# Layer 1's cross-attention in quarters of 512 queries, shorter prologue, ternary sums on TensorE, SiLU a block ahead

## The chip, the cores and the metric

The kernel runs on one core of one Trainium2 chip, in one launch. The metric is the device time of an execution in microseconds (us); what is quoted is the median over several executions. TensorE does matmuls (PE in the profile, PEld its weight loads), VectorE is DVE, ScalarE is ACT, GpSimd is POOL, and SyncE (SP) issues the transfers.

## What is computed

1024 tokens of width 128 (`x`) go through two layers, with a context of 6404 rows of width 96. Every sublayer is `x = layernorm(x + f(x))`.

```
layer 0: linear attention, 16 heads (relu, rms-normed q and k)
         cross-attention on the context, 8 heads of 64, softmax over 6404 keys
         mixture of experts: 64 routed of 88 wide (top 8), 2 shared, silu(x Wg) * (x Wu)
layer 1: attention with rotated q, k, v (1024 x 1024 softmax)
         BitNet cross-attention:
             vis = bit(ctx, W_d2v); img = bit(vis, W_img); fused = bit(x, W_txt)
             for r in (0, 1):                        # two rounds
                 kv = bit(img, W_att[r])             # 6404 x 64
                 k = concat(kv, kv)                  # 6404 x 128
                 attn = softmax(fused k^T / sqrt(128))
                 fused = fused + 0.1 * attn k
             h = relu(bit(concat(fused, mean(img)), W_f1)); out = bit(h, W_f2)
         low-rank experts (top 2 of 8), and a last layernorm
bit(x, W): ws = mean|W|, qW = sign(W) * (|W| > ws / 2); is = max|x| / 127
           out = (round(x / is) @ qW^T) * (ws * is) + b
```

As `k` holds `kv` twice, a round's scores are the product of `kv` with the sum of the two halves of `fused`. A matrix DUP of the kernel, in one matmul, makes that sum and doubles it onto both halves of the 128 rows.

## The kernel before

**Precision.** A float32 product is made of float16 parts (high and low), in three matmuls: low keys by high queries, high by low, high by high. The exponentials and the values are float32, in matmuls that take several passes.

**Scores in place.** The PSUM banks of the scores are not cleared from tile to tile. The keys are stored as differences from the key some tiles before (256 earlier, the constant LAG), so that each matmul adds what turns the last scores into the next. A half begins with "seeds" (L1855), matmuls that put minus the query's maximum into the banks by a diagonal matrix.

**The maximum.** The maximum over the keys is wanted before the exponentials. It is taken over pairs of keys, as (sum + |difference|): TensorE makes both products for 512 or 1024 keys (L1833 and L1838 in a pass "alone", L1917 between other work), ScalarE takes the magnitude (L774 and L778, L815), VectorE adds the two and reduces (L1180). The pass alone is `max_alone`; beside other work it goes step by step, and a step's TensorE part waits for VectorE's of the step before the last.

**Layer 0's cross-attention** runs in eight halves (`hf`, 512 queries by two heads each), in four pairs `p`. A half has 26 units of two key tiles; each tile has scores (L1870) on two bank pairs, exp by ScalarE (L795), values by TensorE (L1885). The sums of the exponentials for the denominators are shared by VectorE (`add_up`, L1230) and GpSimd (L606), GpSimd with a quarter of the columns. Beside this, in "slots", the next pair's sums, keys and values are made (`items_of`, all through bank 5, one item freeing the bank for the next: `FREED_BY`), and its maxima. Layer 1's context path runs beside it too (`CHAIN`, on VectorE; `BIT_AT` lists at which slots of the first pair the ternary weights are made). It has two reductions across partitions by GpSimd: L617 (the sum of the rows' |W| in the first half) and L614 (the maximum `AM` in the third half); they stand between GpSimd's sums of these halves.

**Prologue.** Transfers of x and of the context in 7 chunks; the first linear attention (L1746 to L1767); context high parts by ScalarE (L714), low parts by VectorE (three, L1081) and GpSimd (L569); differences between the two halves of the keys by GpSimd (L562), their rounding by ScalarE (L724); the first LayerNorm; first values, sums and keys through banks 3 to 7 (`K16_EARLY` and `V_EARLY` of them ahead of the queries); then the first maximum alone (L1833).

**Experts.** 46 blocks of 128 rows: 44 of routed experts, 2 of shared. For block n: up and gate matmuls (L2058), SiLU by ScalarE (L928), products by VectorE (L1415, L1421), a float16 high part by ScalarE (L941), the low part by GpSimd (L636), down matmuls. ScalarE's order in the loop is

```
hidden_hi(4 * i + j, j)
silu(4 * i + (1 + j), (1 + j) % 2)
```

**Layer 1's cross-attention** has two rounds. Each: a DUP matmul pair (L2190) of XT, the fused state with features on the partitions; the queries' high part by ScalarE (L1004) and low part by VectorE (L1614); a maximum alone of 26 steps (`ALONE1`), seeds, 26 units of two tiles by 1024 queries with sums on VectorE 1024 wide for each tile; denominators (L1897), reciprocal (L1236), normalization (L1245). Then VectorE scales the four blocks into `OO` (L1632) and adds them to XT (L1636), 1024 wide. Beside the first round the second's keys (`dk`), values and sums ("sides") are made, through banks 6 and 7 and bank 5. GpSimd quantizes the mean of the image embeddings (L648, L649) between all-reduces of the later quantizations; it gives a bias for `h` (L2217). TensorE has 43 matmuls there that only keep it going (L1713).

## Time and profile before

| what | us |
|---|---|
| median of 3 executions (lowest, highest) | 1700.82 (1698.92, 1707.68) |
| profiled execution, its time | 1697.55 |
| profiled execution, its span | 1695.8 |
| TensorE busy in the span | 1547.2 (91%) |
| VectorE busy | 1300.1 (77%) |
| ScalarE busy | 1111.2 (66%) |
| GpSimd busy | 432.4 (25%) |
| mean granted TensorE clock, share of full speed | .938 |

The span is that of the instructions of the core; the execution's time is 1.75 us more. Stages by the trace: prologue to 71.9, layer 0's cross-attention to about 1035, experts from 1052 to about 1270, layer 1's attention and quantizations to 1361.8, its cross-attention to 1640.04 (the last denominators), the tail to 1695.8. In a row, the first number is the start from the start of the span, the second the time that the merged instructions (x8: eight of them) took; in brackets the idle time of the engine before and what ended it.

### The profile page before, as it was taken

To read this page: it belongs to the slowest core of one execution; us is meant where nothing else is said; L and a number is where in the kernel's file an instruction comes from. 1 tells how busy PE (TensorE), PEld (TensorE's weight loads), DVE (VectorE), ACT (ScalarE), POOL (GpSimd) and SP (SyncE) were. 2 spreads that over 40 slices of the span, in tenths; PEclk is the share of its full clock that TensorE was granted. 3 is DMA by queue.
4 is the path that set the end of the run, shared out by engine and by line. 5 is a ranking of instruction groups with operands and counts; after the bars stand their busy time and mean duration, and the time that the engine had idled before them with its cause. 6 is when DMAs were issued, how large, how long until landed. Compare 5 with 4: busy or idle time off the path is not lost.

```text
span 1695.8 us, 26434 instructions
## 1 busy us (share of the span) xinstructions
PE 1547.2 (91%) x9040; PEld 557.2 (33%) x9058; DVE 1300.1 (77%) x2233; ACT 1111.2 (66%) x1490; POOL 432.4 (25%) x407
## 2 busy tenths in 40 slices
PE   6888899999989999999999998999997969978996
PEld 4412223333323333333332333333444612211333
DVE  7798888779877778887788888766665686778775
ACT  5587777767867767877777786655553366746543
POOL 6203433434533434434400010344441000000000
PEclk8758999999999999999999998999999969976998
DMA  4000000000100000000010000111100000000000
GB/s 130 7 1 6 1 1 1 1 2 12 48 8 1 1 2 3 1 1 10 20 33 1 1 1 26 33 43 46 42 23 1 1 1 1 1 0 1 1 13 13
DMA packets 14829, 22.75 MB, mean 13 GB/s; under 512 B 1990, under 2 KB 11766, under 8 KB 14710
## 3 DMA queue, kind: packets, MB, share of 16 engines
q1 hardware_dynamic: 14710, 21.22, 4.5%
q8 instruction: 68, 1.11, 0.3%
q14 instruction: 51, 0.42, 0.1%
HBM read 20.69 MB, written 0.52 MB: 13 GB/s over the span
## 4 chain that ended last, share of the span: by engine, by line
PE 66%; issue 13%; DVE 12%; POOL 5%; ACT 3%; DMA 0%; POOLq 0%; SPq 0%; DVEq 0%; ACTq 0%
PE PS L1885 26%; PE PS L1870 18%; PE PS L1917 5%; POOL WRK L636 4%; DVE KNB L1180 4%; PE PS L1833 3%; PE PS L1739 2%; PE PS L1731 2%; DVE WRK L1230 1%; DVE QS L1236 1%; PE PS L2164 1%; ACT KNB L815 1%; PE PS L2149 1%; PE PS L1855 1%; PE PS L1723 1%
## 5 line engine op out<-in xcount | busy, mean ns | idle before, releaser
L1230 DVE TENSOR_TENSOR WRK<-WRK 128x768 f32<-128x768 f32 (+1 forms) x500 | 549.3, 1099 | 60.2 <-ACT WRK L795 45.2
L795 ACT ACTIVATE WRK<-PS 128x1024 f32<-128x1024 f32 (+1 forms) x510 | 500.0, 1023 | 108.1 <-PE PS L1870 89.9
L1885 PE MATMUL PS<-WRK,V 128*64 128x512 f32 (+1 forms) x2040 | 495.0, 605 | 0.0
L1180 DVE CUSTOM_DVE_ANT_0 KNB<-PS,KNB 128x512 f16<-128x512 f32 (+2 forms) x464 | 331.3, 731 | 127.1 <-PE PS L1917 114.9
L606 POOL TENSOR_TENSOR WRK<-WRK 128x256 f32<-128x256 f32 x300 | 282.3, 941 | 395.5 <-ACT WRK L795 378.3
L815 ACT ACTIVATE KNB<-PS 128x512 f16<-128x512 f32 (+2 forms) x306 | 180.7, 591 | 97.3 <-PE PS L1917 97.2
L2058 PE MATMUL PS<-WRK,KNB 128*128 128x512 f16 x828 | 197.1, 383 | 12.7 <-POOL WRK L636 4.3
L1885 PEld LDWEIGHTS PS<-WRK,V 128*64 128x64 f32 (+1 forms) x2040 | 124.1, 136 | 246.6 <-issue 199.8
L1870 PE MATMUL PS<-Q,KB 64*128 64x512 f16 (+1 forms) x1428 | 192.8, 379 | 0.1
L1870 PE MATMUL PS<-KNB,KB 64*128 64x512 f16 (+1 forms) x1224 | 155.7, 376 | 0.0
L636 POOL TENSOR_TENSOR WRK<-KB,WRK 128x1024 f16<-128x1024 f32 x46 | 98.6, 2144 | 132.6 <-ACT WRK L941 132.6
L2058 PEld LDWEIGHTS PS<-WRK,KNB 128*128 128x128 f16 x828 | 77.1, 98 | 124.0 <-issue 23.4
L774 ACT ACTIVATE KNB<-PS 128x1024 f16<-128x1024 f32 x96 | 98.0, 1024 | 27.0 <-DVE MXP L1180 15.5
L1415 DVE TENSOR_TENSOR KA<-PS,KB 128x1024 f32<-128x1024 f32 x46 | 56.3, 1225 | 72.7 <-ACT KB L928 72.7
L1870 PEld LDWEIGHTS PS<-Q,KB 64*128 64x128 f16 (+1 forms) x1428 | 65.5, 94 | 129.1 <-ACT WRK L795 44.7
L941 ACT ACTIVATE WRK<-KB 128x1024 f16<-128x1024 f32 x46 | 48.6, 1057 | 90.4 <-DVE KB L1421 87.1
L645 POOL PARTITION_ALL_REDUCE AM<-AX x3 | 1.1, 370 | 378.3 <-DVE AX L1641 293.8
L1917 PE MATMUL PS<-KNB,Q 64*128 64x512 f16 (+1 forms) x448 | 79.4, 357 | 17.9 <-DVE MXP L1180 10.0
L1870 PEld LDWEIGHTS PS<-KNB,KB 64*128 64x128 f16 (+1 forms) x1224 | 59.7, 94 | 62.8 <-issue 10.9
L1833 PE MATMUL PS<-CTX,Q 64*128 64x512 f16 x192 | 49.9, 598 | 15.4 <-DVE MXP L1180 7.4
L1870 PE MATMUL PS<-Q,KA 64*128 64x512 f16 (+1 forms) x408 | 62.3, 384 | 0.0
L1833 PE MATMUL PS<-KNB 64*128 64x512 f16 x192 | 49.8, 604 | 11.5 <-DVE MXP L1180 7.2
(347 smaller groups left out, 1532.1 us busy)
## 6 DMA issues: line engine op xcount, KB each, us to landing
V<-in_moe_w_dram SPq DMA_DIRECT2D x44, 192.0 KB, 2.4
KNB<-in_ctx_fm_dram SPq DMA_DIRECT2D x6, 384.0 KB, 8.2
X<-in_ctx_fm_dram SPq DMA_DIRECT2D x12, 192.0 KB, 2.4
CTX<-in_ctx_fm_dram SPq DMA_DIRECT2D x6, 384.0 KB, 3.9
BW<-in_bit_w_dram SPq DMA_DIRECT2D x1, 960.0 KB, 10.0
PWK<-in_pair_w_dram SPq DMA_DIRECT2D x4, 192.0 KB, 2.4
XT<-in_x_fm_dram SPq DMA_DIRECT2D x1, 512.0 KB, 4.6
X<-in_x_tm_dram SPq DMA_DIRECT2D x1, 512.0 KB, 11.6
```

The source lines that it names most:

```text
L606: e.tensor_tensor(total, total, part, ALU.add).then_inc(S("acc_pool"), 1)
L636: e.tensor_tensor(H_LO[hslot], MH[hslot % 2], H_HI[hslot], ALU.subtract).then_inc(S("h_lo"), 1)
L774: e.activation(MC[:, m % 2, :], bank(b, b + 2), ACT.Abs).then_inc(S("x_cp"), 1)
L795: e.activation(PR[0:r, u % 2, b, :], bank(2 * b, 2 * b + 2, slice(0, r)), ACT.Exp).then_inc(S("exp"), 1)
L815: e.activation(MC[:, m % 2, 0:w], PS[:, 6, 0:w], ACT.Abs).then_inc(S("x_cp"), 1)
L1180: return e.tensor_tensor_reduce(diffs, sums, diffs, 0.5, NEG, ALU.add, ALU.max, accum_out=out)
L1230: e.tensor_tensor(total, total, part, ALU.add).then_inc(S("acc"), 1)
L1833: ins = e.matmul(o, queries[rows, tiles[0] * P:(tiles[0] + 1) * P], keys[rows, at:at + HALF], start=True, stop=True)
L1870: ins = e.matmul(PS[0:r, 2 * b + h, :], keys[rows, j * P:j * P + r], queries[rows, q[h]], start=False, stop=(k == 2), skip_group_check=True)
L1885: ins = e.matmul(PS[h * HD:(h + 1) * HD, 4, :], v(r, j, h), PR[0:r, unit_no(hf, i) % 2, b, h * HALF:(h + 1) * HALF], start=(j == 0), stop= ...
L1917: ins = e.matmul(PS[:, b, k * w:(k + 1) * w], QH[(p + 1) % 2][rows, t * P:(t + 1) * P], K16[rows, off + a:off + a + w], start=True, stop=True)
L2058: ins = e.matmul(bank(b + h), w_[:, part, :], rows[:, h * HALF:(h + 1) * HALF], start=start and i == 0, stop=stop and i == 2, skip_group_c ...
```

## The change

It has six parts.

1. **Layer 1's cross-attention in quarters.** The quarter n is round n // 2 and the query half n % 2. A unit of a quarter is two key tiles on the two halves of the rows, by 512 queries. The maximum of the first quarter alone is taken in 13 steps (`ALONE1`); those of the next three in 26 steps of half the width (`STEPS1`) beside the units of the quarter before: in quarter 0 in units 0 to 23, in quarters 1 and 2 in units 7 to 23 (`steps1`), with up to two steps in a unit. There are four buffers for the exponentials (PR1) for two before. Round 1's sides, values and keys go one a unit through bank 5 (`items1_of`). A quarter's denominators, normalization, a DUP matmul on it ("fold") and its addition to half of XT run in the next quarter's units 1 to 4, and the query matmul of the quarter after next in unit 6. GpSimd adds 0.1 times the bias to XT ahead. The keys of layer 1 are differences from 512 earlier.
2. **Prologue.** GpSimd makes all of the context's remainders and two small weight remainders; two groups of first values go early, by banks 6 and 7; first keys go through five banks; fewer sums and values stand ahead of the queries; R's bias is added by GpSimd.
3. **Ternary sums** across partitions by a matmul with ones in slot 12 of the first pair ("bits"), VectorE copies the result. The all-reduce for AM[0] stands after all of GpSimd's sums of layer 0.
4. **The mean** is quantized by VectorE.
5. **Layer 1's text quantization** loses its clamp: two VectorE operations for three.
6. **Experts:** on ScalarE SiLU of block n + 1 stands ahead of the high part of block n.

The core of the diff:

```diff
-ALONE1 = full_then_rest(NDC - 1, lambda t: (t % 2,), 6)
+ALONE1 = [(d, [t], t % 2) for d in range(NDC - 1) for t in range(NT // 2)] + [(NDC - 1, [0, 1, 2, 3], 0)]
...
+    if p == 0:
+        at[12].append(("bits", 0))
     at[27].append(("den", 2 * p))
...
+STEPS1 = [(c, [t], t % 2) for c in range(NFULL) for t in range(NT // 2)] + [(NFULL, [0, 1, 2], 0), (NFULL, [3], 1)]
+NM1 = len(STEPS1)
...
+def steps1(n, i):
+    first, last = (0 if n == 0 else 7), NU - 3
+    if n + 1 == QUARTERS or not first <= i <= last:
+        return []
+    k = last - first + 1
+    return list(range((i - first) * (NM1 + 1) // k, (i - first + 1) * (NM1 + 1) // k))
+def items1_of(n):
+    at = {i: [] for i in range(NU)}
+    if n == 0:
+        for k, x in enumerate(SIDES):
+            at[k].append(("side", x))
+        for k, x in enumerate(NEXT_KV[:NU - len(SIDES)]):
+            at[len(SIDES) + k].append(x)
+    else:
+        at[1].append(("den", n - 1))
+        at[2].append(("den2", n - 1))
+        at[4].append(("fold", n - 1))
+        if n < 3:
+            at[6].append(("query", n + 1))
+        if n == 1:
+            for k, x in enumerate(NEXT_KV[NU - len(SIDES):]):
+                at[0 if k == 0 else 7 + k].append(x)
+    return at
...
-K16_EARLY, V_EARLY = 14, 6
+K16_EARLY, V_EARLY = 12, 5
...
-            q.dma_start(PWK[:, :, :], pair_w[0, :, 0:3, :]).then_inc(S("ld_pwk"), 16)
+                if c == 3:
+                    q.dma_start(PWK[:, :, :], pair_w[0, :, 0:3, :]).then_inc(S("ld_pwk"), 16)
...
             difference(2)
+            remainder(0)
+            remainder(1)
+            e.wait_ge(S("wk_hi"), 1)
+            e.tensor_tensor(WK3[0:DC, 1, :], PWK[0:DC, 1, :], WK3[0:DC, 0, :], ALU.subtract).then_inc(S("wk_lo"), 1)
+            e.wait_ge(S("wv_hi"), 1)
+            e.tensor_tensor(WV2[0:DC, 1, :], PWK[0:DC, 2, :], WV2[0:DC, 0, :], ALU.subtract).then_inc(S("wv_lo"), 1)
             difference(3)
+            remainder(2)
             remainder(3)
             for c in range(4, NKC):
                 difference(c)
...
+            e.wait_ge(S("ln_x"), NT)
+            e.tensor_tensor(R[:, :, :], X_[:, :, :], sm("bo").unsqueeze(1).to_broadcast([P, NT, D]),
+                            ALU.add).then_inc(S("r_bias"), 1)
...
-                    if hf == 2 and i == MAG_DONE + 1:
-                        e.wait_ge(S("ax"), 1)
-                        e.partition_all_reduce(AM[:, 0:1], AX[:, 0:1], P, RED.max).then_inc(S("am"), 1)
-                    if hf == 0 and i == 11:
-                        e.wait_ge(S("bit_rows"), 1)
-                        e.partition_all_reduce(BT[:, 0:7], BR[:, 0:7], P, RED.add).then_inc(S("bit_sum"), 1)
-            for i in range(1, 3):
+            for i in range(3):
                 e.wait_ge(S("ax"), i + 1)
                 e.partition_all_reduce(AM[:, i:i + 1], AX[:, i:i + 1], P, RED.max).then_inc(S("am"), 1)
             link(e.memset(SWAP, 0.0))
             for base in (0, HD, -HD):
                 diag(DUP, base)
             e.sem_inc(S("dup"), 1)
+            for r in range(2):
+                link(e.tensor_scalar(BT1[:, r:r + 1], sm(f"b_att{r}"), 0.1, None, ALU.mult))
             e.wait_ge(S("ln_x"), 2 * NT)
...
             for i in range(3, 6):
+                if i == 4:
+                    add_bias(0, 0, slice(0, T))
...
+                        add_bias(quarter, 1, slice((quarter - 1) * HALF, quarter * HALF))
                 e.wait_ge(S("ax"), i + 1)
                 e.partition_all_reduce(AM[:, i:i + 1], AX[:, i:i + 1], P, RED.max).then_inc(S("am"), 1)
-                if i == 4:
-                    e.wait_ge(S("ws"), 5)
-                    link(e.tensor_scalar(AVG[:, 0:1], AVG[:, 1:2], AI[:, 4:5], MAGIC, ALU.mult, ALU.add))
-                    e.tensor_scalar(AQ[:, :], AVG[:, 0:1], MAGIC, None, ALU.subtract).then_inc(S("avg_q"), 1)
...
-            for c in range(NKC):
+            for c in range(4):
                 context_hi(c)
             k_weights(0)
             v_weights(0)
+            for c in range(4, NKC):
+                context_hi(c)
...
-            e.wait_ge(S("ctx_dve"), DVE_DIFF + DVE_LO)
-            e.wait_ge(S("c_lo"), 1)
+            e.wait_ge(S("c_lo"), 4)
...
                         weights_hi(4 * i + (2 + j), j, 16 * i + (48 if j >= 2 else 16))
+                    silu(4 * i + (1 + j), (1 + j) % 2)
                     hidden_hi(4 * i + j, j)
-                    silu(4 * i + (1 + j), (1 + j) % 2)
...
+                t = turn(n, i)
+                e.wait_ge(S("sc"), BEFORE_SC + t + 1)
+                if t >= len(PR1):
+                    e.wait_ge(S("pv"), BEFORE_PV + t - len(PR1) + 1)
+                    e.wait_ge(S("acc"), BEFORE_SC + t - len(PR1) + 1)
+                b = 2 * (i % 2)
...
+            for n in range(QUARTERS):
                 for i in range(NU):
-                    for b in tiles_of(i):
-                        exp(hf, i, b)
-                    if r == 0:
-                        beside((NEXT_KV, lambda x: kv(1, x)), i, NU)
-                        if i < len(SIDES):
-                            sums_and_differences(1, *SIDES[i], 5)
-                copy_out(hf)
+                    magnitude1(n, steps1(n, i)[0:1])
+                    exp1(n, i)
+                    magnitude1(n, steps1(n, i)[1:])
+                    if i == 0 and n:
+                        copy_out1(n - 1)
+                    for x in ITEMS1[n][i]:
+                        bank5_1(x)
...
-                e.wait_ge(S("c_hi"), c + 1)
-                split_lo(C_LO[0:DC, a:a + w], CTX32[:, a:a + w], C_HI[0:DC, a:a + w]).then_inc(S("ctx_dve"), 1)
-            k_weights(0)
-            v_weights(0)
+            for g in range(2):
+                first_values(g, first_values_bank(g))
...
+                first_values(g, first_values_bank(g))
             q_out(0, 0, 2)
             q_out(0, 1, 7)
             for g in range(V_EARLY, NVG):
-                first_values(g, 3 + g % 3)
-            e.tensor_tensor(R[:, :, :], X_[:, :, :], over_tiles(sm("bo")), ALU.add).then_inc(S("a0_dve"), 1)
+                first_values(g, first_values_bank(g))
             for c in range(NKP):
-                k_out(0, c, 3 + (NVG + c) % 3)
+                k_out(0, c, first_keys_bank(c))
...
                     e.wait_ge(S("bit_sum"), 1)
+                    e.tensor_copy(BT[:, 0:7], PS[:, 5, 0:7]).then_inc(S("bit_dve"), 1)
+                    e.wait_ge(S("bit_dve"), 1)
...
-            quantize(XQ, bank(0, 2), XF, 3).then_inc(S("quant"), 1)
+            link(e.tensor_scalar(XF, bank(0, 2), AI[:, 3:4], MAGIC, ALU.mult, ALU.add))
+            e.tensor_scalar(XQ, XF, MAGIC, None, ALU.subtract).then_inc(S("quant"), 1)
...
+            def add_up1(n, i):
+                t = turn(n, i)
+                e.wait_ge(S("exp"), BEFORE_SC + t + 1)
+                r, w = (P, T) if len(tiles_of(i)) > 1 else (TAIL, HALF)
+                part = PR1[t % len(PR1)][0:r, 0:w]
+                if i:
+                    e.wait_ge(S("acc"), BEFORE_SC + t)
+                    total = ACC[0:r, n % 2, 0:w]
+                    e.tensor_tensor(total, total, part, ALU.add).then_inc(S("acc"), 1)
+                else:
+                    e.wait_ge(S("den_ps"), 2 * PAIRS + n - 1)
...
+            def fold(n):
+                r, u = divmod(n, 2)
+                part = slice(u * HALF, (u + 1) * HALF)
+                e.wait_ge(S("fold"), n + 1)
+                e.wait_ge(S("pre_b"), 1 if r == 0 else 2 + u)
+                e.scalar_tensor_tensor(XT[:, part], bank(5), 0.1, XT[:, part], ALU.mult,
+                                       ALU.add).then_inc(S("fused_upd"), 1)
...
-            e.tensor_tensor(AX[:, 4:5], AVG[:, 2:3], AVG[:, 3:4], ALU.max).then_inc(S("ax"), 1)
+                    maximum1(quarter, steps1(quarter, i)[0:1])
+                    if i:
+                        add_up1(quarter, i - 1)
+                    elif quarter:
+                        add_up1(quarter - 1, NU - 1)
+                    maximum1(quarter, steps1(quarter, i)[1:])
+                    for x in ITEMS1[quarter][i]:
+                        bank5_1(x)
+                    if quarter + 1 < QUARTERS and i == NU - 2:
+                        shifts1(quarter + 1)
...
+            link(e.tensor_scalar(AVG[:, 0:1], AVG[:, 1:2], AI[:, 4:5], MAGIC, ALU.mult, ALU.add))
+            e.tensor_scalar(AQ[:, :], AVG[:, 0:1], MAGIC, None, ALU.subtract).then_inc(S("avg_q"), 1)
...
+                elif kind == "bits":
+                    e.wait_ge(S("bit_rows"), 1)
+                    e.matmul(PS[:, 5, 0:7], ones[:, :], BR[:, 0:7], start=True, stop=True).then_inc(S("bit_sum"), 1)
...
+            def fold(n):
+                e.wait_ge(S("on"), 2 * PAIRS + n + 1)
+                e.matmul(bank(5), DUP, ON[:, n % 2 * HALF:(n % 2 + 1) * HALF], start=True,
+                         stop=True).then_inc(S("fold"), 1)
...
+            def max_steps1(n, steps):
+                base = base1(n)
+                for m in steps:
+                    if m == 0:
+                        e.wait_ge(S("f2_lo"), max(n, 1))
+                        e.wait_ge(S("lk16"), (n // 2 + 1) * 2 * NSC)
+                    if m < NM1:
+                        e.wait_ge(S("x_cp"), base + m)
+                    e.wait_ge(S("mx"), base + m - 1)
+                    if m < NM1:
+                        max_half1(n, m, 0, 6, "x_ps")
+                    if m:
+                        max_half1(n, m - 1, NH, 7, "y_ps")
...
+            for n in range(QUARTERS):
+                if n == 2:
+                    e.wait_ge(S("lk_lo"), 2 * NKP)
+                    e.wait_ge(S("vt_ev"), 2 * NVT)
                 for i in range(NU):
-                    for b in tiles_of(i):
-                        scores(hf, i, b)
+                    max_steps1(n + 1, steps1(n, i)[0:1])
+                    scores1(n, i)
+                    max_steps1(n + 1, steps1(n, i)[1:])
+                    for x in ITEMS1[n][i]:
+                        bank5_1(x)
                     if i:
-                        for b in tiles_of(i - 1):
-                            values(hf, i - 1, b)
-                    if r == 0:
-                        beside((NEXT_KV, lambda x: kv(1, x)), i, NU)
-                        if i < len(SIDES):
-                            sums_and_differences(1, *SIDES[i], 5, 1)
-                values(hf, NU - 1, 0)
-                denominators(hf)
+                        values1(n, i - 1)
+                    elif n:
+                        values1(n - 1, NU - 1)
+            values1(QUARTERS - 1, NU - 1)
+            denominators1(QUARTERS - 1)
+            fold(QUARTERS - 1)
```

## Rows read from the trace of the kernel before

**Rows 1.** The page: the chain that ended last, by engine.

```profile
PE 66%; issue 13%; DVE 12%; POOL 5%; ACT 3%; DMA 0%; POOLq 0%; SPq 0%; DVEq 0%; ACTq 0%
```

**Rows 2.** Windows: busy us (instructions) of PE, PEld, DVE, ACT, POOL; PEclk, DMA, GB/s.

```profile
183.00:189.00 6.00, 5.29 (x34) 1.41 (x30) 5.18 (x10) 4.38 (x7) 1.74 (x3) 1.00 0.00 1
...
1366.00:1400.00 34.00, 25.07 (x112) 4.67 (x112) 30.44 (x65) 27.00 (x28) 0.00 (x0) 0.57 0.00 1
```

**Rows 3.** Timelines (start, us, engine, line) in layer 1's attention; last: a group.

```profile
1369.24 1.22 DVE L1180 CUSTOM_DVE_ANT_0 KNB<-PS,KNB 128x1024 f16<-128x1024 f32 x1
...
1371.74 1.22 DVE L1180 CUSTOM_DVE_ANT_0 KNB<-PS,KNB 128x1024 f16<-128x1024 f32 x1
...
1401.62 1.89 PE L1855 MATMUL PS<-DIAG,ones 128*128 128x512 f16 x4 [2.92 <-DVE DIAG L1207]
...
1502.72 1.08 PE L1897 MATMUL PS<-WRK,ones 128*64 128x512 f32 x4
...
1552.94 1.89 PE L1855 MATMUL PS<-DIAG,ones 128*128 128x512 f16 x4 [2.92 <-DVE DIAG L1207]
...
1629.89 0.39 PE L1870 MATMUL PS<-Q,KB 64*128 64x512 f16 x2
...
1633.16 0.39 PE L1870 MATMUL PS<-Q,KB 64*128 64x512 f16 x2
...
1640.04 1.08 PE L1897 MATMUL PS<-WRK,ones 128*64 128x512 f32 x4
...
L1230 DVE TENSOR_TENSOR WRK<-WRK 128x1024 f32<-128x1024 f32 x24 | 29.4, 1225 | 9.8 <-ACT WRK L795 8.6
```

**Rows 4.** Timelines of TensorE and VectorE in a slot of layer 0.

```profile
183.83 0.39 PE L1917 MATMUL PS<-KNB,Q 64*128 64x512 f16 x2
...
184.06 0.81 PE L1870 MATMUL PS<-KNB,KB 64*128 64x512 f16 x6
...
184.29 0.69 DVE L1180 CUSTOM_DVE_ANT_0 KNB<-PS,KNB 128x512 f16<-128x512 f32 x1 [0.19 <-PE PS L1917]
...
185.13 0.39 PE L1917 MATMUL PS<-KNB,Q 64*128 64x512 f16 x2 [0.27 <-DVE MXP L1180]
...
189.34 0.39 PE L1917 MATMUL PS<-KNB,Q 64*128 64x512 f16 x2
```

**Rows 5.** Timelines of GpSimd and TensorE around the two all-reduces.

```profile
201.69 8.79 POOL L606 TENSOR_TENSOR WRK<-WRK 128x256 f32<-128x256 f32 x8 [7.05 <-issue]
...
205.04 0.39 PE L1917 MATMUL PS<-KNB,Q 64*128 64x512 f16 x2 [3.46 <-issue]
...
496.53 0.71 POOL L606 TENSOR_TENSOR WRK<-WRK 4x256 f32<-4x256 f32 x1 [7.01 <-issue]
...
497.39 1.98 PE L1897 MATMUL PS<-WRK,ones 128*64 128x512 f32 x4 [4.68 <-POOL WRK L606]
```

**Rows 6.** Timelines of TensorE and ScalarE over one expert block.

```profile
1241.22 2.75 PE L2058 MATMUL PS<-WRK,KNB 128*128 128x512 f16 x12 [0.19 <-ACT KB L928]
...
1244.59 1.01 ACT L928 ACTIVATE KB<-PS 128x1024 f32<-128x1024 f32 x1
...
1249.11 1.01 ACT L928 ACTIVATE KB<-PS 128x1024 f32<-128x1024 f32 x1
```

**Rows 7.** Timelines of GpSimd, ScalarE and VectorE in the prologue.

```profile
25.17 5.81 POOL L562 TENSOR_TENSOR WRK<-KNB 96x1024 f32<-96x1024 f32 x3
...
35.79 1.11 ACT L688 ACTIVATE KNB<-PS 128x512 f16<-128x512 f32 x2 [0.95 <-PE PS L1724]
...
35.05 2.21 DVE L1081 TENSOR_TENSOR WK<-PWK,WK 96x128 f16<-96x128 f32 x1
...
37.18 0.76 DVE L1081 TENSOR_TENSOR WV<-PWK,WV 96x128 f16<-96x128 f32 x1
```

**Rows 8.** Timeline of TensorE after layer 1's last denominators.

```profile
1645.23 10.31 PE L1713 MATMUL PS<-BQ,ones_b 128*128 128x512 bf16 x43 [0.22 <-issue]
...
1658.40 0.25 PE L2217 MATMUL PS<-AQ,BQ 128*128 128x1 bf16 x4 [2.86 <-POOL AQ L649]
```

424 lines of the change are left out of this document (285 added, 139 removed).

## The prediction, made before the changed kernel ran

> **What bounds the kernel now.** I read the page first: TensorE is busy 91% of the 1695.8 us, and the chain that ended last runs through it for 66% and through VectorE for 12% [rows 1]. So an edit pays where TensorE waits, or where it loses work or clock. The windows show its granted clock [rows 2], and the timelines of the edited stretches where it waits: layer 1's attention [rows 3], a slot of layer 0 with the maximum beside it [rows 4], GpSimd around its all-reduces [rows 5], an expert's block [rows 6], the prologue [rows 7] and the tail [rows 8]. In the attention TensorE starts work back to back: a unit of 2 key tiles by 1024 queries takes 3.27 us (1629.89 to 1633.16). The time beside that is the two passes for the maximum, 50.2 us for the second with what leads to it (1502.72 to 1552.94). Durations are of one profiled execution of 1697.55 us, 3.3 below the median of 1700.82; I add the sum to the first and put the 3.3 back.
>
> **Layer 1's attention.** The stretches of before are seeds to denominators, 101.1 us (1401.62 to 1502.72) and 87.1 us (1552.94 to 1640.04), with 50.2 between. *Removed:* the second pass alone, and 13 of the first one's 26 steps. Two steps take 2.50 us (1369.24 to 1371.74) [rows 3], so the seeds come 13 x 1.25 = 16.3 us earlier, at 1385.3.
> *Added on TensorE:* 188.2 us of the two stretches stay. 104 half-units replace 51, each of half of that unit's 3.27 us, 1.635, and, my estimate, .055 for the extra changes of tile shape: +5.7. The 78 steps for the next quarter's maximum cost .23 each (183.83 to 184.06, the pair of matmuls [rows 4]): +17.9. Three more denominators of four float32 matmuls, twice the old ones' four passes (1.08 with their fill, .94 each without, by my estimate), 1.87 each: +5.6. The fold of each quarter and the query of two, single float32 matmuls of half of 1.87: 5 x .93 = +4.7. Round 1's keys, values and sides through the one bank 5, where the key pieces must wait for their eviction: +2.5. Waiting for the queries: +1.4. Sum 226.0 us.
> *Added as a wait:* one item's maximum needs TensorE, then VectorE, and TensorE's next step needs the bank back. In a unit with two steps I see this ring: .46 from TensorE's step to VectorE's start (183.83 to 184.29), .62 for the first maximum (.69, less what overlaps with the next instruction) [rows 4], then a 1024-wide sum of 1.15 (1.225 in the group's mean, less the overlap of neighbours [rows 3]), then the second maximum, .84 from its start to TensorE's next step (184.29 to 185.13). 3.07 us, where TensorE's own work in such a unit is 1.69 + 2 x .22 = 2.13. Quarters 1 and 2 have ten two-step units each, as the steps are squeezed into 17 of 26 units: 20 x .94 = 18.8; quarter 0 has three, already longer by their keys: 2.0; and seven key pieces of quarter 1 in the same units .5 each: 3.5. Sum 24.3. Behind the waiting step stand the scores, and behind those the exponentials, so nothing fills it. That layer 0 shows the like speaks for it: a slot with three steps takes 5.51 us (183.83 to 189.34) [rows 4], and TensorE waits in it for the maximum (.27 before 185.13).
> So the last denominators start at 1385.3 + 226.0 + 24.3 = 1635.6 instead of 1640.04: **-4.4**. Were the ring hidden: -28.7.
>
> **Ternary sums by TensorE, AM's first all-reduce later.** GpSimd goes away before each all-reduce and behind it: 7.05 us before its next sum at 201.69, 7.01 before 496.53 [rows 5]. The sum that comes late holds a buffer of the exponentials, so TensorE then waits 3.46 (before 205.04); the second time 4.68 (before 497.39). Removed: 3.5 and 4.7, and an estimated .8 for the matmuls that run slowly behind the second (1.98 us for four of 1.08 [rows 3, 5]). Added: a float32 matmul of 7 columns at slot 12 and VectorE's copy that frees bank 5, for which the key matmul of slot 13 waits; a TensorE-VectorE-TensorE trip like the .84 above, about 1 us. The AM all-reduce now stands behind GpSimd's last sum of layer 0 on its queue; VectorE asks for it one or two slots later, so I cost it at nothing; without that cover it is one spell, 7. Sum **-8**; bounds -11 (all idle gone, clock kept) and 0 (the spell comes back at the fourth pair).
>
> **Experts.** A block takes 4.52 us (SiLU 1244.59 to 1249.11). It is a ring: ScalarE's rounding of block n waits for VectorE, SiLU of n + 1 (1.01) stands behind it, and VectorE's two products wait for SiLU, the four of about the same length, and so the sum of a block [rows 6]. With SiLU of the next block first the ring is open; but TensorE idles just .19 us in a block (before 1241.22), so it binds next at 4.33: 43 x .2 = **-8.6**. Bounds: -11 (the drain shortens too) and +2 (product late by a SiLU, 1.01, for the down matmuls, which stand two blocks behind; only the last block pays).
>
> **Prologue.** GpSimd takes VectorE's three remainders and the small weights' two. Its differences, 5.81 us for three [rows 7], gate ScalarE's halves, and these stand on ScalarE's queue ahead of the sums' evictions (35.79). They end 3 x 1.94 + 2 x .5, 7 us later, or 11 if each of the remainders is half as long again. In return VectorE and ScalarE enter the LayerNorm sooner, five value and key evictions, each a little above half of 1.11 [rows 7], no longer stand ahead of the queries (-3.2), R's bias leaves VectorE's queue and the keys go through five banks. The queries were ready late anyway. The normalization starts .6 late; sum **-1.5**, bounds -3.5 and +4 (the 7 to 11 less those covers).
> The Trainium skill ("SBUF — State Buffer", section "SBUF: two separate sides") has VectorE and GpSimd exclude one another on a shared port for a whole instruction. A 96x128 subtraction of VectorE took 2.21 us beside GpSimd's wide one, the same shape right behind .76 [rows 7], so the trace agrees. By the rule GpSimd alone would be at its short time and the prologue nearer -3.
>
> **Rest.** Layer 1's text quantization loses one of three 1024-wide VectorE passes: -.7. The first key piece of round 0 needs one matmul for three: -.2. Mean quantized by VectorE: the query-independent matmul waited 2.86 us for GpSimd (before 1658.40). But the 43 matmuls that keep the clock up (10.31 us) stand ahead of it [rows 8], and they now start after the last fold. From the last denominators: 2.0 to VectorE, 3.4 for the reciprocals, .7, fold 1.0, transposes 1.1, then 10.3: 18.7 against 18.4 (1640.04 to 1658.40). **+.4**, bounds -3 and +3.
>
> Sum: -4.4 - 8 - 8.6 - 1.5 - .7 - .2 + .4 = -23.0: 1674.6, and 3.3 more for the median, **1678**. Its own range, by the terms' bounds apart from the ring: 1666 to 1690.
>
> **Rivals.** A. *The ring is hidden* (VectorE's maximum slips before the sum, or the four probability buffers absorb it): attention -28.7, time 1653. For: the chain in rows 4 also shows a two-step stretch, and TensorE there is busy 5.29 of 6 us [rows 2]. Against: the 5.51 us slot. Chance .24; a ring half hidden (1666) is the lower end of my case.
> B. *Experts don't gain*, because GpSimd or TensorE's weight loads stand at 4.5 already: 1686. Chance .10.
> C. *The clock falls in the quarters.* With TensorE idle .94 of 3.07 us in ten units running, the granted clock may go to 1.2 GHz, as where the first pass alone runs it shows a mean of .57 with TensorE busy 25 of 34 us [rows 2]. A two-step unit then takes 2 x 2.13 = 4.26, 1.19 more than the ring; in 20, with the one-step units of these quarters (14 x 1.9), +50: 1728. It makes the kernel slower from about two thirds of them (1678 + 33 = 1711). Against: rows 2's stretch at 183 us, clock 1.00 with idle of this size. Chance .07.
> D. *The moved work pays itself back*: the prologue's differences at +4, the all-reduce late by 7 and quarters at +6: 1696 to 1705, no change. .10.
> My case .49. That the change doesn't do what it says is excluded: the diff removes the second pass and both all-reduces.
>
> **How the numbers follow.** Range: from A, less 2 for its other terms (1651), to the near end of D (1694). A measurement of this kernel can tell about .5%, 8.5 us, from no change. Faster holds my case, A and B but for a tail: .81; within .5%: D and that tail, .11; slower: C and what of D exceeds, .08.
>
> **What would show it.** Right: one pass of thirteen wide steps; two-step units of quarters 1 and 2 at about 3.07 us with TensorE's maximum step waiting for VectorE; no idle of 6 to 7 us on GpSimd in pairs 0 and 1, and no exponential waiting over 2 us there; blocks of 4.3 us; the first maximum step near 70.4; the mean's matmul right behind the 43. Wrong: two-step units near 2.2 us (A), blocks of 4.5 (B), a granted clock under .9 in 1420 to 1600 (C), a first maximum step past 74 or a new wait at the fourth pair (D).

## The result and the profile after

The changed kernel takes 1673.73 us (median of 4; 1672.37 to 1674.18), the kernel before beside it 1701.57: the ratio is 0.983, with a 95% interval of [0.9803, 0.9857], 27.8 us less. The forecast was 1678. The profiled execution has a span of 1672.3 us for 1695.8, 23.5 less, where the working had 23.0; the other 4 us lie between that execution of before and the median beside which it is now held.

The page of the changed kernel, its busy times:

```profile
PE 1544.0 (92%) x9078; PEld 556.9 (33%) x9096; DVE 1301.9 (78%) x2306; ACT 1121.4 (67%) x1531; POOL 442.5 (26%) x415
```

TensorE is about as busy as before (1544.0 us for 1547.2) in a shorter span. What went is nearly all waiting. To see where, I read the same landmarks in both traces: when a group of matmuls starts. The last column splits the prediction's terms over the same stretches.

| stretch, by TensorE's landmarks | before | after | difference | forecast |
|---|---|---|---|---|
| start to the first maximum | 71.87 | 68.46 | -3.4 | -1.5 |
| to layer 0's first seeds | 67.00 | 67.00 | 0 | 0 |
| to the 1st denominators (ternary sums) | 118.80 | 118.31 | -.5 | -2.5 |
| to the 4th (AM's all-reduce is in the 3rd) | 373.95 | 368.26 | -5.7 | -5.5 |
| to the 8th | 401.84 | 401.86 | 0 | 0 |
| to the filler behind the experts | 248.30 | 233.87 | -14.4 | -8.6 |
| to the DUP matmuls | 80.02 | 82.14 | +2.1 | -.9 |
| to layer 1's first seeds | 39.84 | 22.99 | -16.9 | -16.3 |
| to its last denominators | 238.42 | 253.37 | +15.0 | +11.9 |
| to the end | 55.76 | 56.04 | +.3 | +.4 |

**The quarters.** Timelines of TensorE and VectorE in the third quarter (start, us, engine, line; they answer to [rows 3, 4]):

```profile
1525.13 0.39 PE L2457 MATMUL PS<-CTX,Q 64*128 64x512 f16 x2
...
1525.59 0.69 DVE L1311 CUSTOM_DVE_ANT_0 KNB<-PS,KNB 128x512 f16<-128x512 f32 x1 [0.16 <-PE PS L2457]
...
1526.21 1.22 DVE L1767 TENSOR_TENSOR WRK<-WRK 128x1024 f32<-128x1024 f32 x1
...
1526.44 0.39 PE L2457 MATMUL PS<-CTX,Q 64*128 64x512 f16 x2 [0.27 <-DVE MXP L1311]
...
1527.35 0.69 DVE L1311 CUSTOM_DVE_ANT_0 KNB<-PS,KNB 128x512 f16<-128x512 f32 x1
...
1528.19 0.39 PE L2457 MATMUL PS<-CTX,Q 64*128 64x512 f16 x2 [0.34 <-DVE MXP L1311]
...
1530.17 0.39 PE L2457 MATMUL PS<-CTX,Q 64*128 64x512 f16 x2
```

From TensorE's first step (1525.13) to VectorE's maximum are .46 us, then .62 to the sum, 1.14 to the second maximum and .84 to TensorE's step of 1528.19: the ring is 3.06 us, and the prediction had 3.07. That closing step is the first one of the next unit, which has one step; the two units together take 5.04 (1525.13 to 1530.17), where the prediction had 3.07 + 1.91. A unit without steps takes 1.76 in the last quarter, where I had 1.69.

**The all-reduces.** GpSimd has none left in layer 0's first five halves; the first stands at 846.3 us, behind its last sum of layer 0. The new item, and the wait for VectorE's copy that it brings to TensorE (.39 and .91 us, 1.3 together):

```profile
189.20 0.39 PE L2162 MATMUL PS<-BR,ones 128*128 128x7 f32 x2
...
194.19 0.39 PE L1925 MATMUL PS<-CTX,WK 96*128 96x512 f16 x1 [0.91 <-DVE BT L1434]
```

**The experts.** The selector matmuls, one pair a block, and ScalarE in the same stretch (they answer to [rows 6]):

```profile
1237.20 0.59 PE L2285 MATMUL PS<-KA 128*128 128x512 f16 x2
...
1241.52 0.59 PE L2285 MATMUL PS<-KA 128*128 128x512 f16 x2
...
1240.42 1.02 ACT L1012 ACTIVATE KB<-PS 128x1024 f32<-128x1024 f32 x1 [0.71 <-PE PS L2262]
...
1241.34 1.05 ACT L1025 ACTIVATE WRK<-KB 128x1024 f16<-128x1024 f32 x1
```

4.32 us a block; SiLU now waits for TensorE (.71 before 1240.42), and the high part follows it. TensorE has no idle left in a block. The last up and gate matmuls, in the drain behind the last block (before, then after):

```profile
1278.82 2.74 PE L2058 MATMUL PS<-WRK,KNB 128*128 128x512 f16 x6 [3.04 <-POOL WRK L636]
```

```profile
1256.24 1.47 PE L2262 MATMUL PS<-WRK,KNB 128*128 128x512 f16 x6 [1.49 <-POOL WRK L712]
```

The wait is 1.55 us shorter, and the six matmuls behind it are 1.27 shorter, as they ran slowly in the kernel before.

**Prologue and tail.** GpSimd and the first maximum step (compare [rows 7]), the tail's filler and the mean's matmul (compare [rows 8]):

```profile
18.38 4.22 POOL L639 TENSOR_TENSOR CTX<-KNB,CTX 96x1024 f16<-96x1024 f32 x2
...
22.56 0.42 POOL L646 TENSOR_TENSOR WK<-PWK,WK 96x128 f16<-96x128 f32 x1
...
30.82 4.80 POOL L632 TENSOR_TENSOR WRK<-KNB 96x1024 f32<-96x1024 f32 x3
...
68.46 1.02 PE L2037 MATMUL PS<-KNB 64*128 64x512 f16 x6 [1.51 <-DVE KB L1217]
...
1625.33 9.81 PE L1915 MATMUL PS<-BQ,ones_b 128*128 128x512 bf16 x43 [0.22 <-issue]
...
1634.97 0.24 PE L2523 MATMUL PS<-AQ,BQ 128*128 128x1 bf16 x4
```

GpSimd's first remainders take 2.1 us each (4.22 for two), the small weight's .42 where VectorE's took 2.21 [rows 7]. The mean's matmul stands right behind the 43.

One edit of the prologue is not in the list of six parts: the reciprocals of the first linear attention's q and k go to PSUM and no longer to SBUF. VectorE's two products with them take 2.35 us for 6.64 (L1273, before L1137). In this profile VectorE then waits 8.39 us for ScalarE ahead of the normalization, so these 4.3 us are not seen to arrive at the first maximum by themselves; no run takes the edit out.

**The clock.** In two places the same matmuls take longer than in the profile of the kernel before: behind the first seeds and behind the experts. In windows of all engines (columns as in [rows 2]), first the kernel before:

```profile
134.00:146.00 12.00, 8.31 (x43) 2.75 (x41) 7.48 (x36) 6.39 (x11) 1.12 (x2) 0.68 0.00 1
...
1281.70:1300.00 18.30, 16.21 (x112) 9.43 (x112) 11.90 (x34) 8.36 (x12) 0.00 (x0) 1.00 0.00 1
...
1300.00:1322.00 22.00, 17.83 (x91) 10.64 (x89) 13.24 (x18) 9.42 (x14) 0.00 (x0) 0.92 0.00 1
...
1345.00:1362.00 17.00, 13.23 (x64) 6.48 (x65) 14.31 (x55) 2.83 (x12) 0.38 (x1) 1.00 0.00 0
```

Then the changed one, whose three windows behind the experts answer to those three:

```profile
134.00:146.00 12.00, 10.54 (x42) 3.50 (x44) 6.59 (x10) 6.66 (x12) 2.16 (x4) 0.70 0.00 0
...
1257.70:1276.00 18.30, 16.52 (x95) 9.25 (x95) 10.30 (x33) 7.58 (x11) 0.00 (x0) 0.91 0.01 1
...
1276.00:1298.00 22.00, 17.39 (x95) 10.03 (x96) 14.21 (x17) 9.54 (x14) 0.00 (x0) 0.92 0.00 1
...
1322.00:1341.00 19.00, 16.38 (x75) 8.46 (x76) 14.55 (x56) 3.88 (x13) 0.38 (x1) 0.91 0.00 0
```

The twelve score matmuls behind the seeds took 1.95 us from 140.66 in the kernel before. Here they, the queries' matmuls and those behind the experts:

```profile
137.26 2.74 PE L2074 MATMUL PS<-KNB,KB 64*128 64x512 f16 x12
...
139.93 2.62 PE L1919 MATMUL PS<-XT,PWK 128*128 128x512 f32 x4
...
1267.44 3.41 PE L2328 MATMUL PS<-XT,RQK 128*128 128x512 f32 x4
...
1284.56 3.45 PE L2368 MATMUL PS<-WRK,XT 128*128 128x512 f32 x4
...
1333.21 4.96 PE L1915 MATMUL PS<-BQ,ones_b 128*128 128x512 bf16 x16
```

2.74 us from 137.26, and the queries behind them 2.62 for 1.98: 1.4 us. The granted clock rises 2.8 us behind the seeds (138.87) in the kernel before and 5.8 behind them (135.46) here. That is not the edit's doing as far as the runs show: in run 3 below, whose prologue is that of the kernel before, it rises 5.7 behind them, and 4.5 to 5.9 in all the other profiles. The profile of the kernel before is the one apart.

Behind the experts four float32 matmuls take 3.41 (1.98 before), four more 3.45 (2.84 before), the filler 4.96 (3.62 before). The granted clock is .91, .92 and .91 in the three windows; in the kernel before it is 1.00, .92 and 1.00, so one of the three falls was there already. The stretch is 2.1 us longer, and with the .7 that the dropped pass should have given it, 2.8 us are lost.

### The profile page after: what moved, and what is told of

It reads as the page before. It is cut to its first block, busy times and chain, and to the rows that moved or that the text cites. A ratio compares the mean times of both kernels' runs of the same rounds, so it can differ in the third digit from the quotient of the medians.

```text
span 1672.3 us, 26773 instructions
## 1 busy us (share of the span) xinstructions
PE 1544.0 (92%) x9078; PEld 556.9 (33%) x9096; DVE 1301.9 (78%) x2306; ACT 1121.4 (67%) x1531; POOL 442.5 (26%) x415
## 4 chain that ended last, share of the span: by engine, by line
PE 63%; issue 14%; DVE 12%; POOL 6%; ACT 4%; POOLq 0%; DMA 0%; DVEq 0%; ACTq 0%; SPq 0%
PE PS L2088 21%; PE PS L2074 14%; POOL WRK L712 5%; PE PS L2120 5%; PE PS L2429 4%; DVE KNB L1311 4%; PE PS L2416 3%; PE PS L1941 2%; PE PS L1933 2%; PE PS L2037 2%; DVE WRK L1361 2%; DVE WRK L1767 1%; PE PS L2457 1%; DVE QS L1367 1%; ACT KNB L898 1%
## 5 line engine op out<-in xcount | busy, mean ns | idle before, releaser
L1361 DVE TENSOR_TENSOR WRK<-WRK 128x768 f32<-128x768 f32 (+3 forms) x400 | 426.9, 1067 | 14.4 <-ACT WRK L878 7.2
L878 ACT ACTIVATE WRK<-PS 128x1024 f32<-128x1024 f32 (+1 forms) x408 | 400.9, 1022 | 52.1 <-PE PS L2074 44.8
L2088 PE MATMUL PS<-WRK,V 128*64 128x512 f32 (+1 forms) x1632 | 395.6, 605 | 0.0
L2088 PEld LDWEIGHTS PS<-WRK,V 128*64 128x64 f32 (+1 forms) x1632 | 99.2, 136 | 194.1 <-issue 158.3
L2074 PE MATMUL PS<-Q,KB 64*128 64x512 f16 (+1 forms) x1224 | 152.6, 377 | 0.0
L1098 ACT ACTIVATE WRK<-PS 128x1024 f32<-128x1024 f32 x100 | 102.3, 1023 | 51.8 <-PE PS L2416 48.4
L1767 DVE TENSOR_TENSOR WRK<-WRK 128x1024 f32<-128x1024 f32 (+1 forms) x100 | 119.8, 1198 | 10.0 <-ACT WRK L1098 8.9
L2429 PE MATMUL PS<-WRK,V 128*64 128x512 f32 (+1 forms) x408 | 111.9, 617 | 0.3 <-DVE MXP L1311 0.3
L2120 PE MATMUL PS<-KNB,Q 64*128 64x512 f16 (+1 forms) x448 | 79.3, 357 | 14.6 <-DVE MXP L1311 10.1
L2074 PEld LDWEIGHTS PS<-Q,KB 64*128 64x128 f16 (+1 forms) x1224 | 55.5, 94 | 89.1 <-ACT WRK L878 21.1
L857 ACT ACTIVATE KNB<-PS 128x1024 f16<-128x1024 f32 x60 | 61.2, 1023 | 16.6 <-DVE MXP L1311 9.5
L1012 ACT ACTIVATE KB<-PS 128x1024 f32<-128x1024 f32 x46 | 47.1, 1023 | 35.7 <-PE PS L2262 35.7
## 6 DMA issues: line engine op xcount, KB each, us to landing
BW<-in_bit_w_dram SPq DMA_DIRECT2D x1, 960.0 KB, 10.1
```

Source lines behind the costliest of these rows:

```text
L878: e.activation(PR[0:r, u % 2, b, :], bank(2 * b, 2 * b + 2, slice(0, r)), ACT.Exp).then_inc(S("exp"), 1)
L1361: e.tensor_tensor(total, total, part, ALU.add).then_inc(S("acc"), 1)
L1767: e.tensor_tensor(total, total, part, ALU.add).then_inc(S("acc"), 1)
L2074: ins = e.matmul(PS[0:r, 2 * b + h, :], keys[rows, j * P:j * P + r], queries[rows, :], start=False, stop=(k == 2), skip_group_check=True)
L2088: ins = e.matmul(PS[h * HD:(h + 1) * HD, 4, :], V[0:r, j, h * HD:(h + 1) * HD], PR[0:r, unit_no(hf, i) % 2, b, h * HALF:(h + 1) * HALF], s ...
L2120: ins = e.matmul(PS[:, b, k * w:(k + 1) * w], QH[(p + 1) % 2][rows, t * P:(t + 1) * P], K16[rows, off + a:off + a + w], start=True, stop=True)
```

## The experiments

Each starts from the changed kernel where nothing else is said, and is held against its 1673.73. That was measured beside 1701.57 for the kernel before. Beside runs 1, 2, 6 and 7 the kernel before took 1700.34, beside 3, 4, 5 and 8 1699.62, and beside 9 1703.26: differences of 2 us and less between medians of different groups show nothing by themselves, and I go by the stages of the profiles there.

**1. Is VectorE's sum in the ring?** The two maxima of a unit ahead of the sum:

```diff
-                    maximum1(quarter, steps1(quarter, i)[0:1])
+                    maximum1(quarter, steps1(quarter, i))
                     if i:
                         add_up1(quarter, i - 1)
                     elif quarter:
                         add_up1(quarter - 1, NU - 1)
-                    maximum1(quarter, steps1(quarter, i)[1:])
```

> The changed kernel, but in a unit with two steps VectorE takes both maxima ahead of the 1024-wide sum. Theory 1 (the sum stands in the ring, as the prediction has it): a two-step unit with the one-step unit behind it takes 5.04 us in the third quarter of the changed kernel; without the sum in the ring TensorE's second step still waits for the first maximum (.46 + .62 + .23 = 1.31 from step to step), so the pair goes to 4.6 to 4.85, 3 to 7 us off the whole, and the seven key units gain most. Theory 2 (VectorE is simply full, or ScalarE's magnitude binds): pair stays at 5.04, total within 1 us. Theory 3 (whole ring gone): pair 4.04 to 4.2, total 15 to 20 us less.

Measured: 1670.83 us, ratio to the kernel before 0.983 [0.9813, 0.9846]. TensorE and VectorE in the third quarter:

```profile
1520.52 0.39 PE L2456 MATMUL PS<-CTX,Q 64*128 64x512 f16 x2
...
1521.98 1.22 DVE L1767 TENSOR_TENSOR WRK<-WRK 128x1024 f32<-128x1024 f32 x1
...
1523.12 0.68 DVE L1311 CUSTOM_DVE_ANT_0 KNB<-PS,KNB 128x512 f16<-128x512 f32 x1
...
1523.96 0.39 PE L2456 MATMUL PS<-CTX,Q 64*128 64x512 f16 x2 [0.42 <-DVE MXP L1311]
...
1525.29 0.39 PE L2456 MATMUL PS<-CTX,Q 64*128 64x512 f16 x2
```

The three steps of a pair of units go from 5.04 to 4.77 us (1520.52 to 1525.29), in the range of the first theory. The sum was in the ring; but taken out of one unit it delays the first maximum of the next (the sum of 1521.98 runs until 1523.12, TensorE's step waits .42). The third quarter, denominators to denominators, goes from 65.17 to 63.71 us, the second stays (68.04 and 68.07): 1.5 us in all, less than the 3 to 7 that I gave, and the key units gain nothing. The rest of the 2.9 lies where nothing was edited: the start (67.58 for 68.46), the stretch from there to the 1st denominators (.6 less) and the one behind the experts (81.46 for 82.14). Against the kernel before beside it, the ratio is that of the changed kernel, .983; so the medians alone don't show this gain, and the 1.5 us rest on one profile of each.

**2. Is the experts' period the ring through ScalarE?** SiLU behind the high part again:

```diff
-                    silu(4 * i + (1 + j), (1 + j) % 2)
                     hidden_hi(4 * i + j, j)
+                    silu(4 * i + (1 + j), (1 + j) % 2)
```

> The changed kernel with the experts' old order on ScalarE (high part of block n, then SiLU of n + 1). Theory 1 (the ring through VectorE and ScalarE made the old period): the spacing of the blocks goes from 4.32 back to a repeating 4.52, 4.52, 4.61, 4.67 (mean 4.58), 11 us over 43 blocks, and the drain behind the last block is 3 us longer; of that 2 us come back behind, if the granted clock in layer 1's attention then has fewer dips: total +12 to +14. Theory 2 (the prediction's size): +8.6. Theory 3 (the period fell because of something else, such as GpSimd): no change.

Measured: 1683.81 us, +10.1, less than the 12 to 14 that the first theory gave; the stretch to the filler is 246.43 us for 233.87, +12.6. Blocks and wait are back:

```profile
1247.69 0.60 PE L2285 MATMUL PS<-KA 128*128 128x512 f16 x2
...
1249.78 2.75 PE L2262 MATMUL PS<-WRK,KNB 128*128 128x512 f16 x12 [0.19 <-ACT KB L1012]
...
1252.36 0.59 PE L2285 MATMUL PS<-KA 128*128 128x512 f16 x2
```

4.67 us here, one of the repeating four (4.52, 4.52, 4.61, 4.67). The 43 periods give 11.0 of the 12.6. The drain gives 1.6, as TensorE waits 3.04 us in it again; the 3 us that I expected of it held another 1.3 for slow matmuls, and here the six behind that wait take 1.47. The stretch behind the filler is 79.59 us for 82.14, 2.5 less: the first four float32 matmuls take 1.98 again and the last filler 3.62.

**3. The same edit alone, on the kernel before.**

> The kernel before with nothing changed but the experts' order on ScalarE (SiLU of block n + 1 ahead of the high part of block n). Theory 1: blocks at 4.32 us for a mean of 4.58, the drain 3 us shorter, 14 us up to the first filler behind the experts, and 0 to 3 us of it lost to a lower granted clock in layer 1's first attention: total -11 to -14. Theory 2 (the prediction's size): -8.6. Theory 3 (the period also needs the other parts): less than 5.

Measured: 1685.59 us beside 1699.62, ratio 0.9909 [0.9893, 0.9924]: -14.0. The stretch to the filler is 234.93 us for 248.30, -13.4, and 80.26 for 80.02 behind it. The first theory holds for the edit. What it said of the clock does not hold as a price of the edit: here the stretch behind the filler lost .2, in the changed kernel 2.8.

**4. Did TensorE wait for GpSimd's all-reduces?** Both back on GpSimd, in the first and third half:

```diff
-        at[12].append(("bits", 0))
...
+                    if hf == 2 and i == MAG_DONE + 1:
+                        e.wait_ge(S("ax"), 1)
+                        e.partition_all_reduce(AM[:, 0:1], AX[:, 0:1], P, RED.max).then_inc(S("am"), 1)
+                    if hf == 0 and i == 11:
+                        e.wait_ge(S("bit_rows"), 1)
+                        e.partition_all_reduce(BT[:, 0:7], BR[:, 0:7], P, RED.add).then_inc(S("bit_sum"), 1)
```

> The changed kernel, but the ternary sums are reduced by GpSimd in the first half again and AM's first all-reduce stands in the third half again. Theory 1 (GpSimd is away for 6 to 7 us before and behind each, and TensorE waits for it): against the changed kernel the first denominators come 1.5 to 2.5 us later, the third's another 4.7 and the fourth's another .9; total +7 to +8.5, GpSimd's rows show 6 us before and 7 us behind each all-reduce. Theory 2 (the old waits had another cause, such as the exponentials' buffers): no such steps, total within 2 us.

Measured: 1682.20 us, +8.5. Around the first all-reduce:

```profile
190.59 0.49 POOL L695 PARTITION_ALL_REDUCE BT<-BR  x1 [5.92 <-issue]
...
198.54 6.16 POOL L684 TENSOR_TENSOR WRK<-WRK 128x256 f32<-128x256 f32 x6 [7.46 <-issue]
...
201.89 0.61 PE L2123 MATMUL PS<-KNB,Q 64*128 64x512 f16 x2 [3.78 <-issue]
...
202.27 2.79 PE L2077 MATMUL PS<-KNB,KB 64*128 64x512 f16 x12
...
205.42 2.90 PE L2091 MATMUL PS<-WRK,V 128*64 128x512 f32 x8
```

```profile
196.00:206.00 10.00, 6.22 (x28) 1.99 (x28) 4.72 (x12) 5.43 (x7) 6.17 (x7) 0.73 0.00 0
```

```profile
196.00:206.00 10.00, 6.54 (x44) 2.05 (x42) 6.36 (x19) 5.11 (x9) 3.73 (x5) 1.00 0.00 0
```

5.9 us before it and 7.5 behind, TensorE waits 3.78, as the first theory has it. But this half costs 3.9 us (122.19 from seeds to denominators for 118.31), more than the 1.5 to 2.5: behind the wait the twelve score matmuls take 2.79 us for 1.46 and the values 2.90 for 1.94, at a granted clock of .73. The second window is that of the kernel before, whose profiled execution kept the clock at 1.00 with its wait of 3.46. That is no property of the kernel: run 3 has the same instructions there, and in its profile TensorE waits 4.75 us, the next twelve score matmuls take 2.79 and the clock is .74 (window 200.1 to 210.1). The third half costs 5.0 and the fourth 1.7 (4.7 and .9 expected). The three halves add to 10.6 us, 2 more than the difference of the medians. In this profile the seeds came .9 earlier, and the stretch behind the experts took 79.46 us for 82.14, with the first four float32 matmuls at 1.98 and the last filler at 3.62, though the experts were not touched. So the 2 to 3 us that the changed kernel loses there hang on more than the experts' order.

**5. What does the prologue owe to the order of its pieces?** 14 and 6 pieces ahead of the queries again:

```diff
-K16_EARLY, V_EARLY = 12, 5
+K16_EARLY, V_EARLY = 14, 6
```

> The changed kernel with 14 sums' pieces and 6 values groups ahead of the queries in the prologue, as before, for 12 and 5. Theory 1 (the prediction's term: five evictions fewer ahead of the queries were worth 3.2 us, three of them by these two numbers): first step of the maximum 1.5 to 2 us later than the 67.6 to 68.7 of the changed kernel's runs. Theory 2 (another chain sets the start, GpSimd's last differences): within .5 us. By either, less than the whole of it reaches the end, if TensorE's clock behind the first maximum is granted in full at about the same time as in the changed kernel.

Measured: 1675.30 us, +1.6. The first maximum step:

```profile
71.55 1.02 PE L2037 MATMUL PS<-KNB 64*128 64x512 f16 x6 [1.51 <-DVE KB L1217]
```

The start of the maximum, 71.55, is near that of the kernel before (71.87, but 70.65 in run 3, whose prologue is the same). It is 3.1 us later than in the changed kernel's profile, and 2.6 to 4.0 later than in all the profiles with 12 and 5 pieces (67.58 to 68.92): more than the 1.5 to 2 of the first theory. So these two numbers carry the gain within about 1 us, and what else the prologue has of new parts nets to little there. Of the 3.1 us 2.8 are left at the 1st denominators; the 1.6 of the medians are within what two groups of runs can differ by.

**6 and 7. What is the mean on VectorE worth?** A filler of 16 matmuls, with the mean on VectorE and, in the second run, with the mean's two operations moved back to GpSimd behind its all-reduce:

```diff
-            keep_busy(44, 2)
+            keep_busy(16, 2)
```

> The changed kernel with 16 in place of 44 filler matmuls ahead of the mean's matmul. Theory 1 (the filler hides what the mean on VectorE gives; the mean is ready at 1628.5 and TensorE comes to it at 1634.97): the tail becomes 5 to 6.5 us shorter, if TensorE's clock is still granted in full for the next matmuls. Theory 2 (the filler is what keeps the clock): the next 15 matmuls run at half the clock, and 2 to 4 us of it are lost again, total -2 to -4.

> As the run with 16 filler matmuls, but the mean is quantized by GpSimd as before. Theory 1: GpSimd's all-reduce ends at about 1626.4, it is away for some 7 us and the mean is ready near 1634, so with the short filler TensorE waits for it and this kernel is within 1 us of the changed one: the move to VectorE is worth nothing beside 44 fillers and 5 to 6 us beside 16. Theory 2 (GpSimd's absence is not from the all-reduce's code): mean ready near 1627, and this run equals the one with 16 fillers.

Measured: 1666.75 us and 1672.48. The mean's matmul and the next ones of the first, then of the second with GpSimd:

```profile
1626.68 0.24 PE L2523 MATMUL PS<-AQ,BQ 128*128 128x1 bf16 x4
...
1626.78 1.89 PE L2533 MATMUL PS<-KB,BQ 128*128 128x512 bf16 x8
```

```profile
1633.01 0.25 POOL L734 TENSOR_SCALAR AVG<-AVG,AI 128x1 f32<-128x1 f32 x1 [7.45 <-issue]
...
1633.67 0.27 PE L2525 MATMUL PS<-AQ,BQ 128*128 128x1 bf16 x4 [5.25 <-POOL AQ L735]
...
1633.81 3.57 PE L2535 MATMUL PS<-KB,BQ 128*128 128x512 bf16 x8
```

From the last denominators to the end the tail takes 49.99 us with VectorE's mean, and 55.91 with GpSimd's, which is 7.45 us away behind its all-reduce; 56.04 in the changed kernel. So the edit is worth 5.9 us beside the short filler. Beside the long one no run has GpSimd's mean, but the times say that nothing would show: it was ready 18.1 us behind the last denominators (1633.67 - 1615.59), and the long filler holds TensorE until 18.7 behind them. Of the 7.0 us that the first run has on the changed kernel 6.0 are in the tail, as its first theory said. The wait of 5.25 us also makes the next matmuls slow (3.57 for 1.89), while the short filler keeps the clock.

**8. Both together.**

> The changed kernel with both maxima ahead of the sum on VectorE and 16 filler matmuls ahead of the mean's matmul. If the two gains are in different stages they add: 2 to 4 us in quarters 1 and 2 and 6 in the tail, 8 to 10 below the changed kernel, near 1664. If the clock spoils one of them, the total is no better than the 1666.75 of the short filler alone.

Measured: 1667.27 us, ratio 0.9802 [0.9788, 0.9815], no better than the 1666.75. The third quarter has its gain (63.71 us), but against run 6 alone the tail took 50.93 us for 49.99, the stretch behind the experts 82.13 for 81.46 and the start 68.92 for 67.70. What is worth 1.5 us disappears in such differences.

**9. Does a wait cost clock behind the experts?** Both, and 11 filler matmuls into TensorE's wait for the diagonal in layer 1's first attention:

```diff
-            e.wait_ge(S("h_max"), NT)
+            e.wait_ge(S("h_max"), NT - 1)
+            keep_busy(11, 1)
+            e.wait_ge(S("h_max"), NT)
```

> The kernel with both maxima ahead of the sum and 16 filler matmuls, plus 11 filler matmuls in layer 1's first attention, where TensorE waits 2.9 us for VectorE's diagonal. In the runs with the experts' new order the float32 matmuls behind that wait took 3.45 to 3.62 us for 1.88, and the filler of the next gap 4.96 to 5.19 for 3.62, at a lower granted clock. Theory 1 (the wait lets the clock fall, and the later arrival is its price): the matmuls behind it take 1.88 again, and the stretch from the first filler behind the experts to the DUP matmuls goes from 81.5 or 82.1 to about 80, total 1 to 2 us below the same kernel without the filler (1667.3). Theory 2 (the fall comes from the drain and the gaps before it): no change, or a fraction later because of the filler.

Measured: 1663.22 us (1661.74 to 1665.35), ratio to the kernel before 0.9776 [0.9762, 0.9789], 4 us less than run 8. Filler, the float32 matmuls behind it, and the filler of the next gap:

```profile
1279.11 2.55 PE L1914 MATMUL PS<-BQ,ones_b 128*128 128x512 bf16 x11 [0.45 <-DVE V L1697]
...
1282.33 1.88 PE L2369 MATMUL PS<-WRK,XT 128*128 128x512 f32 x4
...
1329.17 3.62 PE L1914 MATMUL PS<-BQ,ones_b 128*128 128x512 bf16 x16
```

```profile
1270.00:1300.00 30.00, 26.94 (x169) 16.22 (x172) 20.21 (x23) 14.76 (x20) 0.00 (x0) 1.00 0.00 1
```

1.88 us for 3.43 in run 8, then 3.62 for 4.98, clock 1.00, and the stretch takes 78.06 us for 82.13. More than the 1 to 2 that I expected, as the later fall went too. A part is not the filler's: the four float32 matmuls ahead of it take 1.98 us here and 3.40 in run 8. In run 6 they took 1.98 as well, and the stretch 81.46; against that the filler is worth 3.4. This is the fastest kernel of the study, 10.5 us below the changed one.

## Why the prediction held, and where its terms did not

The forecast of 1678 with a range of 1651 to 1694 was right. That the sum of the profile comes so near (-23.0 for -23.5) is luck: three terms are off by more than 2 us and cancel, and both profiles carry clock differences of 1 to 3 us that no term had. The range of 1666 to 1690 named beside the sum is not that of its bounds either: added up, the upper ones give 1705.

- *Layer 1's attention* (-4.4 forecast, -1.9 measured). The step "1385.3 + 226.0 + 24.3" holds in its mechanism: passes -16.9 for -16.3, ring 3.06 for 3.07, pair 5.04 for 4.98; run 1 shows by taking the sum out that it stood in the ring. Mis-sized was the unit: .055 for the changes of tile shape is .13 (1.76 for 1.635). On the 84 units that the ring doesn't bound that is some 6 us by estimate, and the quarters are 3.1 longer than forecast, so other terms gave half of it back; which ones, no run separates. Rival A, the ring hidden, is out. So is C: the granted clock is .98 in the first quarter and 1.00 in the other three. The stretch that the prediction held against C (5.29 us busy of 6) had less idle than these quarters (60.76 busy of 67 in the second), so it was a weak reason for a right guess.
- *Ternary sums and AM* (-8 forecast). In the two profiles -6.2, with the clock's late rise (+1.4) inside; in run 4's medians -8.5, and by its stages -10.6, of which the clock behind the first wait is a part. The cost of the new item is 1.3 us, about as expected. The late all-reduce cost nothing, as expected: from the 4th to the 8th denominators both kernels take the same. What I left open is the price of the clock behind a wait; I had it for the second wait alone, and run 4 has it behind the first too.
- *Experts* (-8.6 forecast, -14.4 in the profiles, -14.0 alone in run 3). The step that failed is "TensorE idles just .19 us in a block". I took the block of 1244.59 as all blocks; every fourth took 4.67 and the one before it 4.61. The 43 periods from the first pair of selector matmuls to the last took 196.7 us and now take 185.6, 11.0 less. The drain, 3.0 us, was in my bound only: 1.55 of it are TensorE's wait for GpSimd (1.49 for 3.04), 1.27 the slow matmuls behind it. The ring and its next bound (TensorE's own 4.32) were right; rival B is out by run 2.
- *Prologue* (-1.5 forecast, -3.4 measured). The term of the five evictions (-3.2) comes near in sum and was mis-sized for one: run 5 puts three of the five back and is 3.1 us later, where the term has 1.9 for three. The step that failed is the delay that I set against it, 7 to 11 us of GpSimd's differences and "The normalization starts .6 late": the differences ended 4.6 later (35.6 for 31.0) and the normalization started 1.8 sooner (41.77 for 43.59). Three of the four remainders ahead of them took 2.1 us, for 3.1 in the kernel before; the fourth took 3.1, beside VectorE's sum of two SBUF tiles (L1295). The Trainium skill's rule of the shared port ("SBUF — State Buffer", "SBUF: two separate sides"), which pointed to -3, agrees with the small weights' .42 us on GpSimd for 2.21 on VectorE, and its number was the better one. In the kernel before both of VectorE's small subtractions ended about .15 us behind a remainder of GpSimd (37.26 behind 37.11, 37.94 behind 37.80), so the .76 us of the second is no free time either. No run separates the port from the order, so it is not shown to be the cause.
- *Text quantization and first key piece* (-.9 forecast, +2.1 for the stretch). The -.7 is there: where the filler ahead takes the same 3.62 us, from its start to the DUP matmuls are 6.01 us (run 2) for 6.75. But the clock fell in that stretch, and run 9 takes 3.4 to 4 us out of it with a filler. That no step of mine had.
- *Tail* (+.4 forecast, +.3 measured). The mean's matmul stands 18.7 us behind the last denominators, the number forecast. That is luck in part: the six terms written for it (2.0, 3.4, .7, 1.0, 1.1, 10.3) add to 18.5, which is +.1. The 43 matmuls do hide the mean's edit, as said at runs 6 and 7, where it is worth 5.9 us.

Something like rival D happened: 1.4 and 2.8 us lie against the gains in these two profiles, but to the clock, not to the waits that I had named, and the late rise of the clock behind the 1.4 is there in run 3 with the old prologue too.

## What to carry to other kernels

Take the period of a loop over as many passes as it is unrolled, not from one: the block that I read could give .2 us, and the mean of four gave .26. When a wait is removed from one engine, look for filler work that still holds the old time; it can hide the gain entirely, and it is the first thing to shorten. And price a wait of TensorE of about 3 us or more with what the matmuls behind it take: that was nothing behind the 3.46 us of the kernel before, and 2.3 us behind the 3.78 of run 4 (2.79 for 1.46 and 2.90 for 1.94).
